# A fused token, attention and expert kernel on one core: the issue order of all five engines is replaced by another

## The reference

```python
q_feat = bilinear_sample(feature_map, ref)             # 1024 grid points a batch
h   = gelu(layer_norm(q_feat @ W_o1 + b_o1, ln_g, ln_b))
off = (h @ W_o2 + b_o2).reshape(B, Nq, 8, 2) * 4.0      # 8 sample points for each
sampled = bilinear_sample(feature_map, ref + off * scale)
keys, values = sampled @ W_k.T, sampled @ W_v.T         # softmax over the 8 points
h = concatenate([tokens, txt], axis=1)                  # 1152 tokens of 64 channels
h = h + causal_attention(layernorm(h))                  # one head, 1152 x 1152
h = h + layernorm(h' + top2_of_16_experts(h'))          # h' = layernorm(h), F = 128
```

## Time and profile before

| | us |
|---|---|
| runs shown | 4560.54, 4563.92, 5620.5 |
| median | 4563.92 |
| the profiled execution, span from first to last instruction | 6851.9 |
| busy: PE, DVE, ACT, POOL | 4265.1, 3165.0, 2222.4, 3077.1 |
| granted clock of PE, mean | 0.734 of 2.4 GHz |

### The profile page before, as it was taken

How to read it: one execution, slowest core, us unless ns; L and a number is a source line. 1 busy time by engine, 2 the same in 40 slices (tenths; PEclk the granted TensorE clock), 3 DMA queues, 4 the chain that set the end, 5 groups by cost and what they waited for, 6 DMA issues and landing times.

```text
span 6851.9 us, 83914 instructions
## 1 busy us (share of the span) xinstructions
PE 4265.1 (62%) x26592; PEld 3681.7 (54%) x26592; DVE 3165.0 (46%) x10220; ACT 2222.4 (32%) x5378; POOL 3077.1 (45%) x3089
## 2 busy tenths in 40 slices
PE   3566765657566575665766667565765757656664
PEld 2555655646455464654656556454654646545543
DVE  1455445354454534545354544534545454544521
ACT  1333332323333332332333323333333333322321
POOL 2554454444534445354454544445344444545331
PEclk9777777777767776786777767777777777767765
DMA  6754443635536354353545536254353545433122
GB/s 194 216 154 136 145 135 115 177 96 157 148 103 189 86 174 119 118 165 94 175 118 160 144 106 190 84 176 119 118 164 93 175 113 152 138 106 89 54 59 67
DMA packets 938637, 911.33 MB, mean 133 GB/s; under 512 B 121306, under 2 KB 822362, under 8 KB 938072
## 3 DMA queue, kind: packets, MB, share of 16 engines
q1 hardware_dynamic: 805768, 598.22, 30.0%
q0 software_dynamic: 132432, 307.74, 15.5%
HBM read 583.69 MB, written 323.53 MB: 132 GB/s over the span
## 4 chain that ended last, share of the span: by engine, by line
another core or an unknown queue 31%; PE 29%; DVE 14%; issue 13%; ACT 10%; SPq 1%; DMA 1%; POOL 0%; DVEq 0%; POOLq 0%; ACTq 0%
PE ps L867 4%; PE ps L881 4%; PE ps L1024 3%; PE ps L1032 3%; PE ps L812 3%; PE ps L964 3%; PE ps L942 2%; ACT rows L1048 2%; ACT xm L1128 2%; DVE prod L1229 1%; PE ps L954 1%; PE ps L1006 1%; PE ps L823 1%; ACT kv_sb L1048 1%
## 5 line engine op out<-in xcount | busy, mean ns | idle before, releaser
L758 POOL DMA_INDIRECT gath<-table,idx x2048 | 2048.2, 1000 | 2909.6 <-issue 1211.3
L881 PE MATMUL ps<-w_kv,samp_t 128*128 128x128 f32 x4096 | 702.9, 323 | 166.6 <-issue 88.1
L867 PE MATMUL ps<-const,prod 128*128 128x128 f32 x4096 | 684.4, 322 | 168.8 <-issue 81.7
L964 PE MATMUL ps<-v_sb,probs_t 128*128 128x64 f32 x2880 | 455.2, 307 | 476.9 <-issue 223.1
L881 PEld LDWEIGHTS ps<-w_kv,samp_t 128*128 128x128 f32 x4096 | 637.0, 234 | 201.0 <-issue 130.5
L964 PEld LDWEIGHTS ps<-v_sb,probs_t 128*128 128x128 f32 x2880 | 442.9, 229 | 544.2 <-issue 303.5
L867 PEld LDWEIGHTS ps<-const,prod 128*128 128x128 f32 x4096 | 596.5, 172 | 202.7 <-issue 152.4
L774 POOL DMA_INDIRECT xs_d<-xm,row x512 | 525.9, 1027 | 392.7 <-DVE row L1229 231.6
L790 POOL DMA_INDIRECT ya<-ys_d,row x512 | 493.4, 964 | 454.4 <-DMA ys_d<-yx 268.6
L1229 DVE TENSOR_TENSOR prod<-gath,corner_w 128x1024 f32<-128x1024 f32 x512 | 619.9, 1219 | 159.3 <-remote 70.6
L942 PE MATMUL ps<-k_t,q_t 128*128 128x512 f32 (+3 forms) x960 | 479.7, 592 | 181.6 <-ACT v_sb L1048 76.5
(11 more groups left out here) (171 smaller groups left out, 6593.0 us busy)
## 6 DMA issues: line engine op xcount, KB each, us to landing
table<-rows SPq DMA_DIRECT2D x224, 1024.0 KB
fm<-in_x SPq DMA_DIRECT2D x256, 512.0 KB
wx<-w_d SPq DMA_DIRECT2D x768, 128.0 KB
gath<-table,idx POOLq DMA_INDIRECT x2048
wx<-w_d SPq DMA_DIRECT2D x64, 512.0 KB
table<-rows SPq DMA_DIRECT2D x32, 960.0 KB
xg<-xs_d SPq DMA_DIRECT2D x192, 130.0 KB
ys_d<-yx SPq DMA_DIRECT2D x192, 128.0 KB
```

Source lines behind the costliest of these rows:

```text
L758: pool.indirect_dma_start(out=gath[:, n % NG, p, :], out_offset=None, in_=tables[par], in_offset=bass.IndirectOffsetOnAxis(ap=idx[:, par, ...
L867: last = pe.matmul(bank(0, p * P, p * P + P), prod[h][:, (p * 2 + dx) * P:(p * 2 + dx + 1) * P], ident, is_transpose=True, start=(dx == 0) ...
L881: last = pe.matmul(bank(1, p * P, p * P + P), samp_t[n % 2][:, (4 * h + p) * P:(4 * h + p + 1) * P], w_kv[:], start=True, stop=True)
L964: last = pe.matmul(bank(7, (i % 8) * C, (i % 8) * C + C), probs_t[n % 3][:, (k % 4) * P:(k % 4) * P + P], v_sb[:, k, :], start=(k == 0), s ...
```

## The change

The strings of all five engines in `TURNS` and `LAST` are replaced. The same letters occur equally often in each (in `TURNS` 56 for SP, 80 for POOL, 286 for PE, 257 for ACT, 463 for DVE), so that each engine does the same stages, on the same tiles, in another order. No stage, buffer, semaphore or transfer is changed. POOL's line of the diff, and one of DVE's:

```diff
     "gpsimd":
-        "pppppppffffffffffffffffpppffffffffffffffffccccccccccccccccccccccccccccccccpppppp",
+        "pppppppppfffffffpffffpfffffpffffffffffffffffccccccccccccccccccccccccccccccccpppp",
     "vector":
-        "wawaaxawwaaaaaaaaaaawvvxwwvvaaxvvwaavvvvvvxavavxaavwaawaavxvvvavawxwavvvaxaavvvwwvvavvvvaxvvvvaawaav"
+        "aaaaaaaaaaaaaaawwxwwwvvvvvvvvxwawawvvvvvvvvxaawaawaaaawxvvvvvvvvawaaaawaxvwvvvvvvvaawaaaaxwvvvvwxvvv"
```

62 lines of the change are left out of this document (31 added, 31 removed).

## The result

| | median us | lowest and highest | runs |
|---|---|---|---|
| before | 4569.76 | 4560.54, 5620.5 | 4 |
| changed | 5390.55 | 5384.53, 5397.15 | 4 |

The run of 5620.5 us, far above the others of the same kernel, is left out of the ratio. The ratio is 1.1799, its 95% interval 1.1775 to 1.1823: 18% slower, where 8.5% was forecast. The direction came out as forecast, the size is more than twice as large, and 5390 lies above the range's end of 5300.

The account below looks back on a forecast made before the run. POOL's indirect DMAs (240 us a period) were taken to bound the kernel before, and the index loop (286 us) the changed one. 4564 + 364 (13 periods) + 40 (first two) - 20 (end) = 4948, rounded to 4950 us, range 4590 to 5300.

Parts of the forecast that it names:

- The mechanism, the bound and the direction: Loop from `idx_ok` through POOL's gathers and fetches, `combine` and DVE back to `idx_ok`: 284 us, above POOL's 240; slower.
- The period before: Timed period of the kernel before: 253 to 263 us, taken as 258, within about 18 us of POOL's 240 us floor.
- "faster" rival: New order avoids PE's late results, which fill the 18 us above POOL's floor; loop under 240 us: 4340 us, chance 0.10.
- What waits within the DVE part ... I add 2 us, from 0 to 25: Waits for PE's results between first-batch `combine` and `idx_ok`: 2 us added to the loop, upper end the 22.90 us stall.
- at most 18 us are lost a period: Timed period 258 less POOL's 240 us: most that PE's late results could cost before; used to keep DVE's waits near 2 us.
- 136 x 1.25 = 170 us: POOL's part of the changed loop: 120 gather DMAs of 15 tiles and 16 fetches, at a step of 1.25 us.
- The 13 periods: Full periods k = 2 to 14 at 286 us against 258, 28 us more each: 364 us (221 to 676).
- The first two periods: Periods without `combine`, index chain's end behind tile 15's weighing: 203 and 217 us, +40 for both (0 to 60).
- The end: Pair 14's 32 scatters no longer ahead of the last two tiles: half of 40 us off, -20 (0 to -40).
- "slower still" rival: PE's late results hit the loop's DVE part at full size: period 307 to 330, 5220 to 5500 us; chance 0.10 above 5250.
- The main case: The index loop sets the period: 4950 us, own range 4700 to 5250, chance 0.65.
- The traced execution: Profile of the kernel before, 6851.9 us against a median of 4563.92, period 420 us; a loop of 286 costs nothing there.

Follow-up runs that it names:

- the pair of kernels with the 12 reductions: Changed kernel plus 12 unused DVE reductions a period, behind first-batch `combine` (inside the loop): 5582.74 us; behind tile 10's weighing (outside): 5420.63 us.
- the timed kernel without it: Changed kernel with the last stretch (`LAST`) of the kernel before, only the periods' order new: 5350.2 us, ratio 1.1697.
- either half alone, and both: Kernel before with DVE's index chain late: ratios 1.0244 to 1.0385; with gathers 11 and 12 ahead of POOL's first-batch fetches: 1.0064; with both: 1.0482 and 1.0568.

## Why the prediction came out as it did, point by point

**The mechanism, the bound and the direction** were right; the terms of the sum were too small, one of them above all. Gather 0 waits for `idx` in 15 pairs, `combine` of the first batch starts 2.5 us behind the start of its last fetch, and the pair of kernels with the 12 reductions shows that this loop sets the time.

**The period before.** 258 us was derived, 262.3 is measured. Not 18 but 22 us lay between it and the 240 us of POOL. What fills them was read wrongly: not PE's late results but POOL's lengthened DMAs (17 us), and some 6 us of waits. With that the "faster" rival has no object. One step that made 258 too small is the count of 15.8 periods between the first gather and the last: the first two take 430.8 us together (gather 0 at 122.0, 298.5 and 552.8), not twice a full period, which leaves (4223.4 - 122.0)/262.3 = 15.6.

**The term that was mis-sized most: "What waits within the DVE part ... I add 2 us, from 0 to 25".** In the period shown the busy time of its 382 instructions is 109.46 us where 112 was taken for instructions and the short gaps between them, but the part lasts 136.3, so DVE is idle for 27 us. 20 of these are waits that the profile names, the rest gaps too short for it. The durations of the 382 add up to 125.0 us, so instructions overlap by some 15 us in all, as the two of the earlier trace rows do; the 118 us that the prediction weighed for a sum without overlap was too low, since its 0.310 us each is covered time too. The longest groups in that stretch, changed (us in total, times, longest):

```profile
DVE yx L1230 <- PE ps L1033: 10.2, 6, 6.7
DVE kq L1230 <- ACT kv_sb L1049: 2.8, 1, 2.8
DVE out_sb L1230 <- ACT out_sb L1129: 2.0, 1, 2.0
```

They are ordinary waits for PE and ACT, in many small pieces, 10.2 us of them for the experts' products. The granted clock is 0.81 there against 0.89 in the same part before, which explains little: a matmul of this part takes 102.39/712 = 0.144 us against 81.56/581 = 0.140. They are no late updates: the whole execution has one wait without a named releaser, of 2.2 us. The argument "at most 18 us are lost a period" was about POOL, and it was used as a bound for DVE, which had slack of its own before and has none now. In the stretch of before DVE is idle for 96.3 - 87.6 = 8.7 us. Over the 13 periods the part lasts 133.1 us on average and not 112 + 2: 19 us a period, 13 x 19 = 250. This is within the bounds of 0 to 25 us that the prediction gave the term, and far from the 2 us that went into the sum.

**POOL's part of the loop: "136 x 1.25 = 170 us".** It took (2402.41 - 2223.53)/135 = 1.325 us a step, and 181.4 us with the landing (181.7 on average) instead of 172. That is 10 us a period, some 126 in all. The 1.25 were read from 16 fetches beside which DVE stood still for 22.90 us, so that nothing could lengthen them. The Trainium skill, "SBUF — State Buffer", section "SBUF: two separate sides", says that GpSimd can't write descriptors while VectorE runs an operation in a 2-port mode. The trace agrees that DMAs are held up, and not on the operations: here it is TENSOR_TENSOR with both operands in SBUF, behind which they end 0.82 us late, with a mean of 1046 ns of the gathers against the usual 946. The same page, under "Who interferes with whom", says that `tensor_tensor` has no such mode, contends only with GpSimd's reads and did not stall DMA in its test; for these indirect DMAs the measurement decides. The prediction priced the effect at 95 us and left it out. In the loop's 136 DMAs it is 137.74 - 136 x 0.946 = 9 us a period, some 118 in all, so it was there, at a little more than that price.

**The 13 periods.** (315.7 - 262.3) x 13 = 695 us instead of 364: DVE's part +19, POOL's +10 and 1 from the indices to gather 0 make +30 on 286; the period before +4 the other way.

**The first two periods.** 111 us instead of 40. The step "POOL's gathers 0 to 15 take 160 us ... some 41 us" was too short on both counts: the first took 241.5 us from gather 0 to gather 0 and not 203, the second 284.7 and not 217. Both terms were too small: POOL's gathers 0 to 15 take 171 and 181 us from the first to the last start, not 160, and from there to `idx` it is 69.5 and 102.5 us where the prediction had the landing and 41 and 55. In that stretch DVE has 175 and 248 instructions, busy for 49.5 and 76.1 us, while 41 and 55 us are some 140 and 190 instructions at the 0.293 us of the sum.

**The end.** +11 us in the profiles, +40 by the timed kernel without it, instead of -20. The scatters did leave the way to the last gathers, which start some 87 us earlier, but what follows the last gather takes 442 us and not 341.

**The rivals.** 5390 lies in the span of 5220 to 5500 that the "slower still" rival gave (its upper end comes to 5520 by its own terms), but not for its reason: no late result of PE stands in the loop. The main case named the cause and missed the size; what put the time over 5300 is the sum of terms that all came out on the high side.

**The traced execution.** It was read as a slow profile of a fast kernel. By its waits without a named releaser and its length it is an execution of the second level, which the same kernel has on four of the five chips with a number on record. The estimate from its durations was sound, the one from its waits wasn't. That the change would cost nothing there was said in the prediction and is borne out (1.0059), although not because a loop of 286 us lay hidden.

**What stays open.** How the loss at the level of 4567 is shared between POOL's order and DVE's index chain, and what of the end's loss each string of `LAST` makes. The kernels that would show the first (either half alone, and both) ran only on chips of the other level, eleven runs in all. That the halves add up within one loop is seen there, in the waits at both of its ends; at the level of 4567 it is argued from the rows, and not shown. Nor is it known why one chip hands PE's updates on at once and four don't.

## What to carry to other kernels

When an order of work is changed, look for the closed loops: from a release through an engine's queue, to a landing, through another engine's queue, and back to the same release a period later. Add their durations and compare with the busiest engine; then charge the loop the ordinary small waits as well, since an engine without slack pays each of them, and for this one DVE's idle time was 27 of 136 us. Before trusting a profile's waits, see that its span is near the timed runs; if not, only its durations hold. To test such a loop, put a known amount of idle work at two places of one engine: it must cost all of itself in one and nothing in the other.

## What the runs showed of the hardware

The same kernel takes 4567 us on one chip and 6829 to 7007 on four others. In the second case DVE and ACT get results late while POOL issues indirect DMAs in a row. In the one case followed up to PE's own row, DVE took the result 15 us after PE had written it, 5.9 us after the last of 40 DMAs. In that trace waits without a named releaser last up to 42.4 us, and those over 8 us end within 6.5 us of a row's last DMA or while the row still goes on. DVE's busy time is the same (3282.9 us in the changed kernel there, 3282.0 here). An order that was made for this lateness won nothing there (1.0059) and lost 18% where it is absent.

An indirect DMA of POOL that starts during a DVE product with both operands in SBUF ends some 0.82 us after it and so takes up to 1.06 us more (2007 ns the longest, 946 in the middle). With the reductions it does not happen: of 330 DMAs that started within a `prod`, 283 took over 1.1 us, and of 185 that started within a reduction of the point attention, none. Over the kernel before this made 2048 x (1.046 - 0.946) = 205 us of POOL's gathers, and POOL is what bounds it.
